# Attention in groups of 256 queries instead of 512: the order of first pass, turns and transfers in a transformer layer

## The chip, the cores and the metric

One core of one Trainium2 chip runs the kernel. The metric is the device time of one execution in microseconds; the kernel before takes 524.16 us, the median of three runs (523.96 to 524.35). The engines are TensorE (PE; its weight loads stand as PEld), VectorE (DVE), ScalarE (ACT), GpSimd (POOL) and SyncE (SP), which here only issues transfers.

## What is computed

The reference, cut to what matters. The input has 2 batches of 1024 positions of 512 features.

```python
def layer(x):                       # (2, 1024, 512)
    qk = (x @ Wqk.T + bqk).reshape(b, n, 8, 8, 2)   # 8 heads of 8 features
    q, k = qk[..., 0], qk[..., 1]
    v = x @ Wv.T + bv
    attn = softmax(q @ k.T) / sqrt(64)              # 1024 x 1024 per head
    x = layernorm(x + (attn @ v) @ Wo.T + bo)
    g, u = x @ Wg.T, x @ Wu.T                       # int4 weights, scales per 128 inputs, 1792 wide
    return layernorm(x + (silu(g) * u) @ Wd.T)
```

## The kernel before

**Blocks and groups.** The 2048 queries are four blocks of 512. Eight heads fall into two groups of four, so there are 8 attention groups of 512 queries and four heads; each goes over 1024 keys in 8 steps of 128 keys, 64 steps in all (`ALL`).

**First pass.** Softmax needs the largest score of each query first. A unit (L911) multiplies 128 queries of one head by 512 keys into one of three PSUM banks, the ring, and VectorE reduces it to a maximum per query (L1198). There are 256 units, 32 for a group (`FG`). When a group's units are done VectorE combines the two halves of the keys (L1206), GpSimd splits the maxima into three half-precision parts (L537), TensorE turns them into rows (a turn "M", L927), ScalarE copies these out of PSUM (L736), and SP moves them into the query operand (`max_rows`, L421), where they are subtracted within the scores product itself. The scores of a group wait for that transfer (L988).

**Second pass.** A step n has two pairs. A pair is two scores products (L981), of two heads at once on two halves of TensorE's rows, and one exponential of 1024 columns (L721). The AV product of the step before (L1017) follows in two halves of 256 columns. Scores alternate between two pairs of PSUM banks, and all "turns" take one of these places too: the maxima's turn M, the turn of a finished group's AV product (avT, behind a copy, L724), which VectorE then normalises (L1216), that of the attention (attT) and the output projection (wo). `turns_at` (L262) says at which step each stands.

**How the two passes run together.** Before the first step TensorE does `AHEAD` = 46 units; then each pair brings two more (L1060 to L1067). So units run out at step `DRAIN` = 53 of 64, and the rest of the loop takes the work of blocks 1 and 2 that was set aside (`ASIDE`, L282): their attention turns and output projections, added by VectorE (L1288). Ahead of the first step TensorE also has, by the hand-written list `later` (L1051), the projections of batch 1 in 12 chunks (L847, L857) and the placement of batch 0's query and key rows: 12 products (L895) that sort features by head, each followed by a ScalarE copy into the stack (L705). The second 512 queries of batch 0 and all rows of batch 1 are placed by transfers instead (`place_second_half`, L412; `place_rows`, L345).

**Queues.** Each engine does its instructions in order. SP: the inputs, the second half's queries, row transfers of groups 0 and 1, batch 1's placements, x's first half, and so on (L436 to L480). GpSimd: fills and constants, splits of the maxima, the scaling of batch 1's queries and keys into high and low parts (L552), half of batch 1's placements, bias additions to x, and the loads of the feed-forward weights, each of which waits for a group's rows to land (L563).

**Behind attention.** VectorE normalises block 0's rows, GpSimd splits them in two half-precision parts, SP transposes them by transfer (L459), and the feed-forward starts (L1126); its first gate product waits for these transposes, for the additions set aside and for the normalisation. SP's transposes stand behind the store of the down-projection's scale ratios, which VectorE computes (L1269). The feed-forward of the other blocks follows period by period without a break.

## Time and profile before

| | |
|---|---|
| median of 3 runs | 524.16 us |
| the profiled execution, its span | 523.78 us, 521.7 us |
| mean granted TensorE clock | 0.992 of full speed |
| TensorE, VectorE, ScalarE, GpSimd busy | 498.3, 413.5, 405.8, 247.9 us |
| 256 first-pass reduces (L1203) | 157.1 us busy |
| 128 exponentials (L721) | 140.6 us busy |
| feed-forward gate, up and down products (L1084, L1096, L1111) | 115.5, 115.3, 131.5 us busy |

Busy time is the union of an engine's instructions. Times in rows count from the span's start. A bracket behind a row is the time that the engine sat idle before it, and who ended that. A row with xN merges N instructions that follow one another. Beside SP stands the time in which it issues transfers; their landing is later.

### The profile page before, as it was taken

To read this page: it belongs to the slowest core of one execution; us is meant where nothing else is said; L and a number is where in the kernel's file an instruction comes from. 1 tells how busy PE (TensorE), PEld (TensorE's weight loads), DVE (VectorE), ACT (ScalarE), POOL (GpSimd) and SP (SyncE) were. 2 spreads that over 40 slices of the span, in tenths; PEclk is the share of its full clock that TensorE was granted. 3 is DMA by queue.
4 is the path that set the end of the run, shared out by engine and by line. 5 is a ranking of instruction groups with operands and counts; after the bars stand their busy time and mean duration, and the time that the engine had idled before them with its cause. 6 is when DMAs were issued, how large, how long until landed. Compare 5 with 4: busy or idle time off the path is not lost.

```text
span 521.7 us, 8074 instructions
## 1 busy us (share of the span) xinstructions
PE 498.3 (96%) x2976; PEld 192.6 (37%) x2976; DVE 413.5 (79%) x706; ACT 405.8 (78%) x558; POOL 247.9 (48%) x288
## 2 busy tenths in 40 slices
PE   8899999999999999999999999999999999999991
PEld 3222232322222222334444444444444444444440
DVE  3699999989999996368778778777668666677677
ACT  1523789998899889877888888888888888888860
POOL 9100091833100625072564686656874834637744
PEclk9999999999999999999999999999999999999996
DMA  6510018675620007400031121130020020000202
GB/s 191 158 45 9 18 42 210 193 142 108 105 44 1 3 5 180 183 0 1 1 62 21 21 41 21 29 54 1 1 80 1 0 82 0 2 1 1 80 0 80
DMA packets 30006, 28.93 MB, mean 55 GB/s; under 512 B 19472, under 2 KB 21904, under 8 KB 29712
## 3 DMA queue, kind: packets, MB, share of 16 engines
q1 hardware_dynamic: 26544, 22.40, 15.2%
q0 software_dynamic: 3424, 6.03, 6.4%
q8 instruction: 23, 0.38, 0.3%
q14 instruction: 15, 0.12, 0.1%
HBM read 24.10 MB, written 4.22 MB: 54 GB/s over the span
## 4 chain that ended last, share of the span: by engine, by line
PE 85%; DVE 7%; ACT 5%; issue 2%; DMA 1%; POOLq 0%; DVEq 0%; POOL 0%; SPq 0%; ACTq 0%
PE ps L1084 18%; PE ps L1096 18%; PE ps L1111 18%; PE ps L1029 9%; PE ps L1000 6%; PE ps L924 6%; DVE mxh L1203 4%; ACT pbuf L721 3%; PE ps L853 3%; PE ps L1012 1%; PE ps L863 1%; PE ps L977 1%; PE ps L907 1%; DMA arena<-xT 1%; ACT avt L728 1%
## 5 line engine op out<-in xcount | busy, mean ns | idle before, releaser
L1203 DVE TENSOR_REDUCE mxh<-ps 128x1 f32<-128x512 f32 x256 | 157.1, 681 | 6.5 <-PE ps L924 5.1
L721 ACT ACTIVATE pbuf<-ps,gamma 128x1024 f32<-128x1024 f32 x128 | 140.6, 1115 | 16.1 <-PE ps L1000 11.2
L802 ACT ACTIVATE ps<-ps,ratio 128x512 f32<-128x512 f32 x168 | 106.5, 659 | 40.3 <-PE ps L1084 37.3
L1111 PE MATMUL ps<-wd,stack 128*128 128x512 f16 x448 | 131.5, 379 | 0.7 <-POOL stack L643 0.7
L1368 DVE TENSOR_TENSOR ps<-ps,stack 128x512 f32<-128x512 f32 x128 | 88.2, 695 | 36.1 <-PE ps L1111 34.3
L1084 PE MATMUL ps<-arena,wg 128*128 128x512 f16 x448 | 115.5, 379 | 0.1
L1096 PE MATMUL ps<-arena,wu 128*128 128x512 f16 x448 | 115.3, 379 | 0.1
L808 ACT ACTIVATE ps<-ps,ratio 128x512 f32<-128x512 f32 x156 | 98.9, 659 | 5.5 <-PE ps L1096 1.1
L641 POOL CAST stack<-pbuf 128x512 f16<-128x512 f32 x56 | 34.2, 611 | 91.6 <-DVE pbuf L1352 91.6
L1368 DVE TENSOR_TENSOR ps<-ps,pbuf 128x512 f32<-128x512 f32 x80 | 55.0, 696 | 23.2 <-PE ps L1111 22.4
L1029 PE MATMUL ps<-pbuf,arena 128*32 128x256 f32 x832 | 66.5, 391 | 1.7 <-ACT avt L728 1.7
L643 POOL TENSOR_TENSOR stack<-pbuf,stack 128x512 f16<-128x512 f32 x56 | 64.8, 1158 | 4.5
L1111 PEld LDWEIGHTS ps<-wd,stack 128*128 128x128 f16 x448 | 43.7, 98 | 54.0 <-POOL stack L643 1.3
L1084 PEld LDWEIGHTS ps<-arena,wg 128*128 128x128 f16 x448 | 43.2, 98 | 54.9 <-ACT pbuf L816 1.7
L1096 PEld LDWEIGHTS ps<-arena,wu 128*128 128x128 f16 x448 | 43.7, 98 | 53.3 <-DVE pbuf L1352 2.0
L924 PE MATMUL ps<-stack 64*128 64x512 f16 x256 | 60.8, 381 | 1.4 <-DVE mxh L1203 0.7
L543 POOL CAST mp<-mx 128x16 f16<-128x16 f32 x8 | 1.6, 197 | 107.5 <-DVE mx L1213 107.5
L1000 PE MATMUL ps<-stack 64*128 64x512 f16 x256 | 49.6, 386 | 1.9 <-ACT pbuf L721 1.6
L1352 DVE SCALAR_TENSOR_TENSOR pbuf<-ps,scales,pbuf 128x512 f32<-128x512 f32 x56 | 41.9, 748 | 6.6 <-PE ps L1096 6.5
L816 ACT ACTIVATE pbuf<-ps,scales 128x512 f32<-128x512 f32 x56 | 38.1, 680 | 0.2 <-PE ps L1084 0.2
L1000 PEld LDWEIGHTS ps<-stack 64*128 64x128 f16 x256 | 12.3, 92 | 58.2 <-issue 37.5
L924 PEld LDWEIGHTS ps<-stack 64*128 64x128 f16 x256 | 20.9, 94 | 34.2 <-DVE mxh L1203 31.2
(112 smaller groups left out, 368.5 us busy)
## 6 DMA issues: line engine op xcount, KB each, us to landing
arena<-xT SPq DMA_DIRECT2D x16, 256.0 KB, 5.4
x<-x SPq DMA_DIRECT2D x2, 2048.0 KB, 9.4
out<-x SPq DMA_DIRECT2D x3, 1024.0 KB, 4.2
stack<-down_ratios SPq DMA_DIRECT2D x1, 2048.0 KB, 7.4
wg<-gq POOLq DMA_DIRECT2D x4, 448.0 KB, 7.4
wu<-uq POOLq DMA_DIRECT2D x4, 448.0 KB, 7.3
wd<-dq POOLq DMA_DIRECT2D x2, 896.0 KB, 10.5
pbuf<-down_ratios SPq DMA_DIRECT2D x1, 1536.0 KB, 6.1
```

The source lines that it names most:

```text
L643: nc.gpsimd.tensor_tensor(mparts[:, 1, t % NM, :], sg[t % 2], mparts[:, 0, t % NM, :], ALU.subtract)\
L721: nc.scalar.activation(pbuf[:, pi % 4, :].rearrange("p (a n) -> p a n", a=2), ps[:, at:at + 2, :], ACT.Exp, scale=gamma[:, n // (ALL // B) ...
L802: nc.scalar.activation(gbank[t % 2], gbank[t % 2], ACT.Copy, scale=gr[:, t % G, c:c + 1])\
L808: nc.scalar.activation(ubank[t % 2], ubank[t % 2], ACT.Copy, scale=ur[:, t % G, c:c + 1])\
L924: nc.tensor.matmul(ring_bank("first", n), qs[b][rows, k, t, qt * P:(qt + 1) * P], ks[b][rows, t, half * TB:(half + 1) * TB], start=True, s ...
L1000: mm = nc.tensor.matmul(bank[at + j], ks[b][rows, t, kt * P:(kt + 1) * P], qs[b][rows, k, t, :], start=True, stop=True)
L1029: mm = nc.tensor.matmul(bank[AVB][j * VC:(j + 1) * VC, lo:hi], vst[b][:, kt, g * HG + j, :], pbuf[:, (2 * n + j // 2) % 4, (j % 2) * TB + ...
L1084: mm = nc.tensor.matmul(gbank[t % 2], wg[:, c, i * P:(i + 1) * P], x1v[blk][:, a, c, :, :], start=(c == 0 and a == 0), stop=(a == 1), skip ...
L1096: mm = nc.tensor.matmul(ubank[t % 2], wu[:, c, i * P:(i + 1) * P], x1v[blk][:, a, c, :, :], start=(c == 0 and a == 0), stop=(a == 1), skip ...
L1111: mm = nc.tensor.matmul(bank[k], mparts[:, a, t % NM, k * P:(k + 1) * P], wd[:, i, :], start=(i == 0 and a == 0), stop=(a == 1), skip_grou ...
L1203: nc.vector.tensor_reduce(mxh[:, f % 2, qh, half:half + 1], ring_bank("first", n), AX.X, ALU.max)\
L1368: nc.vector.tensor_tensor(dst, bank[k], down_row(i), ALU.mult).then_inc(s_dr[k], 1)
```

## The change

Groups become 256 queries: 16 groups of 16 units, each over 1024 keys in 4 steps of 256 keys, 64 steps as before. The scores of a pair become four products of 256 columns, an AV call sums 128 keys for all 256 queries. Attention starts behind 30 units, the first pass ends at step 57 of 64. There are 16 turns of the maxima, each of four row transfers of half the size; the AV turns stay 8, each of two groups, normalised together. The query and key rows of heads in the last two positions of batch 0's first 512 queries are placed by 32 transfers (keys on SP, queries on GpSimd) instead of 6 products and copies, into memory that GpSimd clears first. x is loaded by GpSimd's queue, its bias added in eighths, the feed-forward weights in six parts. On SP batch 1's placements stand behind group 2's rows, and on VectorE the order behind the first pass is new. The diff, cut to its core:

```diff
-NG = H // HG
-STEPS = NG * KT
+QB = 2
+QT = BT // QB
+QN = TB // QB
+GROUPS = H // HG * QB
+NF = NB * GROUPS
+TURNS = NF // QB
+KS = KT // 2
+STEPS = GROUPS * KS
...
-FG = HG * BT * 2
-FIRST = NB * NG * FG
+MQ = HG * QT
+FG = 2 * MQ
+FIRST = NF * FG
...
-            f, r = divmod(n + 3, KT)
-            if r == 0 and f < NB * NG:
+            f, r = divmod(n + 3, KS)
+            if r == 0 and f < NF:
...
-            f, r = divmod(n - 9, KT)
-            if r == 0 and 0 <= f < LASTF:
-                return [("avT", f, 0)]
+            a, r = divmod(n - 10, QB * KS)
+            if r == 0 and 0 <= a < TURNS - 1:
+                return [("avT", a, 0)]
...
-            if r == 2:
+            if r == 3:
...
-        WO_AT = (3, 4)
-        LASTF = NB * NG - 2
-        DRAIN = ALL - 11
-        ASIDE = {DRAIN: ("attT", 1, 0), DRAIN + 1: ("wo", 1, 0), DRAIN + 3: ("wo", 1, 1), DRAIN + 4: ("avT", LASTF, 0),
-                 DRAIN + 6: ("attT", 2, 0), DRAIN + 7: ("wo", 2, 0), DRAIN + 9: ("wo", 2, 1)}
+        WO_AT = (4, 7)
+        DRAIN = ALL - 7
+        ASIDE = {DRAIN: ("attT", 1, 0), DRAIN + 1: ("wo", 1, 0), DRAIN + 2: ("wo", 1, 1), DRAIN + 3: ("attT", 2, 0),
+                 DRAIN + 4: ("wo", 2, 0), DRAIN + 5: ("wo", 2, 1)}
...
-        copied = [use for use in aside for _ in range({"avT": 0, "attT": 1, "wo": 2}[use[0]])]
+        copied = [use for use in aside for _ in range({"attT": 1, "wo": 2}[use[0]])]
...
-        placed = [use for t in range(TH) for use in ((1, 0, t), (0, 0, t), (1, 1, t))]
+        placed = [use for t in range(2) for use in ((1, 0, t), (0, 0, t), (1, 1, t))]
...
+        def place_last_heads(engine, kind):
+            for jj in range(2):
+                for part in range(2):
+                    at = kind * HD + jj * HD // 2
+                    for slot in range(4)[half_slots(kind, part)]:
+                        r = ROWS * jj + E * slot
+                        for t in range(2, TH):
+                            src = (high, low)[part][at + t:at + HD // 2:TH, :]
+                            if kind:
+                                engine.dma_start(ks[0][r:r + E, t, :], src).then_inc(s_late[kind], 16)
+                            else:
+                                engine.dma_start(qs[0][r:r + E, 0, t, :], src[:, 0:TB]).then_inc(s_late[kind], 16)
...
             def max_rows(f):
-                u, g = divmod(f, NG)
+                u, q4 = divmod(f, GROUPS)
+                g, h = divmod(q4, QB)
...
-                for jj in range(2):
-                    r = ROWS * jj + MROW
-                    sp.dma_start(qs[b][r:r + 3, k, 2 * g:2 * g + 2, :],
-                                 mrows[6 * BT * jj:6 * BT * (jj + 1), f % 2, :]).then_inc(s_mld[g], 16)
-            sp.wait_ge(s_fill, 7)
+                for c in range(HG):
+                    r, t = ROWS * (c // 2) + MROW, 2 * g + c % 2
+                    sp.dma_start(qs[b][r:r + 3, k, t, h * QN:(h + 1) * QN],
+                                 mrows[3 * QT * c:3 * QT * (c + 1), f % 2, :]).then_inc(s_mld[q4], 16)
+            sp.wait_ge(s_fill, 11)
...
+            place_last_heads(sp, 1)
+            max_rows(0)
...
-            max_rows(0)
...
+            max_rows(2)
...
-            sp.dma_start(x1[:, 0:8, :], x[0:8].rearrange("t p n -> p t n")).then_inc(s_x[0], 16)
-            max_rows(2)
-            for jj in range(2):
-                sp.wait_ge(s_stk1[jj], 16 * PARTS)
-            sp.wait_ge(s_vt, B)
-            sp.dma_start(x1[:, 8:16, :], x[8:16].rearrange("t p n -> p t n")).then_inc(s_x[1], 16)
-            max_rows(3)
             def turn_x1(u):
...
-            for f in range(4, NB * NG):
+            for f in range(3, NF):
...
-                if f == 5:
+                if f == 10:
...
+            nc.gpsimd.memset(qs[0][:, 0, 2:TH, :].bitcast(F32), 0.0).then_inc(s_fill, 1)
+            nc.gpsimd.memset(ks[0][:, 2:TH, :].bitcast(F32), 0.0).then_inc(s_fill, 1)
+            pool.wait_ge(s_fill, 9)
+            for jj in range(2):
+                r = ROWS * jj + MROW
+                nc.gpsimd.memset(ks[0][r:r + 3, 2:TH, :].bitcast(F32), MINUS_ONES).then_inc(s_fill, 1)
...
-            pool.wait_ge(s_fill, 6)
+            pool.wait_ge(s_fill, 11)
+            pool.wait_ge(s_high, 1)
+            pool.wait_ge(s_low, 1)
+            place_last_heads(pool, 0)
             def second_batch_parts():
...
+                for late in s_late:
+                    pool.wait_ge(late, 16 * 16)
...
             def load_weights(f):
-                pool.wait_ge(s_mld[f % NG], 16 * 2 * (f // NG + 1))
-                if f == 2:
-                    for c in range(C):
-                        pool.dma_start(wg[:, c, :], gq[c]).then_inc(s_gu, 16)
-                if f == 3:
-                    for c in range(C):
-                        pool.dma_start(wu[:, c, :], uq[c]).then_inc(s_gu, 16)
-                if f == 4:
-                    for g in range(0, G, G // 2):
-                        pool.dma_start(wd[:, g:g + G // 2, :], dq[g:g + G // 2].rearrange("g p n -> p g n"))\
-                            .then_inc(s_dq, 16)
+                pool.wait_ge(s_mld[f % GROUPS], 16 * HG * (f // GROUPS + 1))
+                half, kind = (f - 4) % 2, (f - 4) // 2
+                if kind < 2:
+                    for c in range(2 * half, 2 * half + 2):
+                        pool.dma_start((wg, wu)[kind][:, c, :], (gq, uq)[kind][c]).then_inc(s_gu, 16)
+                else:
+                    own = slice(half * G // 2, (half + 1) * G // 2)
+                    pool.dma_start(wd[:, own, :], dq[own].rearrange("g p n -> p g n")).then_inc(s_dq, 16)
...
+            def load_x(b):
+                if b:
+                    for half in s_stk1:
+                        pool.wait_ge(half, 16 * PARTS)
+                    pool.wait_ge(s_vt, B)
+                own = slice(b * N // P, (b + 1) * N // P)
+                pool.dma_start(x1[:, own, :], x[own].rearrange("t p n -> p t n")).then_inc(s_x[b], 16)
...
+            load_x(0)
+            split_max(2)
...
+            split_max(3)
...
             def add_attention(u, t):
...
-                pool.wait_ge(s_xb, u * TB // N + 1)
+                pool.wait_ge(s_xb, 2 * (u + 1))
...
-            def add_bias(b):
+            def add_bias(i):
...
-                pool.wait_ge(s_x[b], 16)
-                half = x1[:, b * N // P:(b + 1) * N // P, :]
-                nc.gpsimd.tensor_tensor(half, half, bo_s.unsqueeze(1).to_broadcast([P, N // P, D]), ALU.add)\
-                  .then_inc(s_xb, 1)
-            for f in range(2, NB * NG):
+                pool.wait_ge(s_x[i // BT], 16)
+                two = x1[:, 2 * i:2 * i + 2, :]
+                nc.gpsimd.tensor_tensor(two, two, bo_s.unsqueeze(1).to_broadcast([P, 2, D]), ALU.add).then_inc(s_xb, 1)
+            for f in range(4, NF):
...
-                if f == 2:
-                    add_bias(0)
-                if f in (2, 3, 4):
+                for i in {4: (0,), 5: (1,), 6: (2,), 10: (3,), 12: (4, 5), 13: (6,), 14: (7,)}.get(f, ()):
+                    add_bias(i)
+                for t in {7: (0, 1), 8: (2, 3)}.get(f, ()):
+                    add_attention(0, t)
+                if 4 <= f < 10:
...
-                if f == 6:
-                    add_bias(1)
-                if f == 3:
-                    for t in range(BT):
-                        add_attention(0, t)
+                if f == 9:
+                    load_x(1)
...
             def av_out(f):
-                act.wait_ge(s_av, 2 * (f + 1) * KT)
+                act.wait_ge(s_av, 2 * (f + 1) * KS)
...
-                    act.wait_ge(s_of, turn_count["avT", f - 2, 0])
-                nc.scalar.activation(avt[:, f % 2, :], bank[AVB], ACT.Copy).then_inc(s_ave, 1)
+                    act.wait_ge(s_of, turn_count["avT", f // QB - 1, 0])
+                h = f % QB
+                nc.scalar.activation(avt[:, f % 2, :], bank[AVB][:, h * QN:(h + 1) * QN], ACT.Copy).then_inc(s_ave, 1)
             def first_max_out():
...
-                nc.scalar.activation(mrows[:, 0, :], ring_bank("M", 0)[0:3 * HG * BT, :].bitcast(F16)[:, 0:P],
...
-            for n in range(4, 9):
+            for n in range(4, 6):
...
-            for n in range(9, 11):
-                keep(n)
...
-            keep(11)
...
-                    if pair and n and n % KT == 0:
-                        av_out(n // KT - 1)
+                    if pair and n and n % KS == 0:
+                        av_out(n // KS - 1)
...
-            av_out(NB * NG - 1)
+            av_out(NF - 1)
...
-                    pe.wait_ge(s_kept, 3 * t + 2 + half)
+                    if t < 2:
+                        pe.wait_ge(s_kept, 3 * t + 2 + half)
+                    else:
+                        for late in s_late:
+                            pe.wait_ge(late, 16 * 16)
...
             def scores(n, pair):
...
-                g, kt = divmod(s, KT)
+                q4, kp = divmod(s, KS)
+                g, h = divmod(q4, QB)
...
-                if kt == 0 and pair == 0:
-                    pe.wait_ge(s_mld[g], 16 * 2 * (u + 1))
+                if kp == 0 and pair == 0:
+                    pe.wait_ge(s_mld[q4], 16 * HG * (u + 1))
...
-                for j in range(2):
-                    rows, t = slice(ROWS * j, ROWS * (j + 1)), 2 * g + pair
-                    mm = nc.tensor.matmul(bank[at + j], ks[b][rows, t, kt * P:(kt + 1) * P],
-                                          qs[b][rows, k, t, :], start=True, stop=True)
+                for kk in range(2):
+                    kt = 2 * kp + kk
+                    for j in range(2):
+                        rows, t = slice(ROWS * j, ROWS * (j + 1)), 2 * g + pair
+                        mm = nc.tensor.matmul(bank[at + j][:, kk * QN:(kk + 1) * QN], ks[b][rows, t, kt * P:(kt + 1) * P],
+                                              qs[b][rows, k, t, h * QN:(h + 1) * QN], start=True, stop=True)
...
-            def av_whole(n):
+            def av(n, kk):
...
-                mm.then_inc(s_av, 2)
-            def av(n, half):
-                u, s = divmod(n, STEPS)
-                g, kt = divmod(s, KT)
-                b = u * TB // N
+                q4, kp = divmod(s, KS)
+                g, h = divmod(q4, QB)
+                b, kt = u * TB // N, 2 * kp + kk
...
-                if kt == 0 and n:
-                    pe.wait_ge(s_ave, n // KT)
-                lo, hi = half * TB // 2, (half + 1) * TB // 2
+                if kp == 0 and n:
+                    pe.wait_ge(s_ave, n // KS)
...
-                    mm = nc.tensor.matmul(bank[AVB][j * VC:(j + 1) * VC, lo:hi], vst[b][:, kt, g * HG + j, :],
-                                          pbuf[:, (2 * n + j // 2) % 4, (j % 2) * TB + lo:(j % 2) * TB + hi],
-                                          start=(kt == 0 and half == 0), stop=(kt == KT - 1), skip_group_check=True)
+                    lo = (j % 2) * TB + kk * QN
+                    mm = nc.tensor.matmul(bank[AVB][j * VC:(j + 1) * VC, h * QN:(h + 1) * QN], vst[b][:, kt, g * HG + j, :],
+                                          pbuf[:, (2 * n + j // 2) % 4, lo:lo + QN],
+                                          start=(kt == 0), stop=(kt == KT - 1), skip_group_check=True)
...
-            later = {1: [(put, 3)], 3: [turn_v], 5: [(put, 4)], 7: [(put, 5)], 9: [(put, 6)], 11: [second[0]],
-                     13: [(put, 7)], 15: [second[1]], 17: [second[2]], 19: [(put, 8)], 21: [second[3]], 23: [second[4]],
-                     25: [(put, 9)], 27: [second[5]], 29: [second[6]], 31: [(put, 10)], 33: [second[7]], 35: [second[9]],
-                     37: [(put, 11)], 40: [second[10]], 42: [second[8]], 44: [second[11]], 46: [second[12]]}
+            later = {0: [(put, 3)], 2: [turn_v], 4: [(put, 4)], 6: [(put, 5)], 8: [second[0]], 10: [second[1]],
+                     12: [second[2]], 13: [second[3]], 15: [second[4]], 17: [second[5]], 18: [second[6]], 20: [second[7]],
+                     23: [second[9]], 25: [second[10]], 26: [second[8]], 28: [second[11]], 30: [second[12]]}
...
-                av_whole(n - 1)
-            av_whole(ALL - 1)
+                for kk in range(2):
+                    av(n - 1, kk)
+            for kk in range(2):
+                av(ALL - 1, kk)
...
-                nc.vector.tensor_tensor(mx[:, f % 2, :], mxh[:, f % 2, :, 0], mxh[:, f % 2, :, 1], ALU.max)\
+                nc.vector.tensor_reduce(mx[:, f % 2, :], mxh[:, f % 2, :, :], AX.X, ALU.max)\
...
-                if n == 38:
+                if n == 24:
...
-            for n in range(ALL):
+            for n in range(DRAIN):
...
-            for k in range(BT):
+            for k in range(2):
+                attention_stats(0, k)
+            att_out(1)
+            for k in range(2, BT):
...
-            att_out(1)
-            down_ratios()
+            normalise(TURNS - 2)
...
+            for t in range(2, BT):
+                add_output(1, t)
+            att_out(2)
+            down_ratios()
+            for t in range(2):
+                add_output(2, t)
...
-                add_output(1, t)
-            normalise(LASTF)
-            att_out(2)
-            for t in range(BT):
```

## Rows read from the trace of the kernel before

**Rows 1.** Page, part 2: TensorE's busy tenths in 40 equal slices of the span

```profile
PE   8899999999999999999999999999999999999991
```

**Rows 2.** Stretches: us; busy us of PE, PEld, DVE, ACT, POOL (instructions); clock; DMA; GB/s

```profile
130.00:140.00 10.00, 9.54 (x98) 2.79 (x91) 9.65 (x17) 9.23 (x11) 1.93 (x2) 1.00 0.48 71
...
200.00:210.00 10.00, 9.75 (x70) 2.48 (x68) 4.34 (x9) 9.49 (x11) 2.64 (x3) 1.00 0.93 266
```

**Rows 3.** Timeline, VectorE's reduces: at the start of attention, and one unbroken run

```profile
51.27 2.48 DVE L1203 TENSOR_REDUCE mxh<-ps 128x1 f32<-128x512 f32 x4 [0.31 <-PE ps L924]
...
68.32 8.46 DVE L1203 TENSOR_REDUCE mxh<-ps 128x1 f32<-128x512 f32 x14 [0.31 <-PE ps L924]
```

**Rows 4.** Timeline behind the last reduce, and the transposes' issues (lowest/median/highest)

```profile
188.44 0.17 DVE L1213 TENSOR_TENSOR mx<-mxh 128x16 f32<-128x16 f32 x1
...
191.63 0.27 DVE L1272 TENSOR_TENSOR stack<-stack 128x112 f32<-128x112 f32 x1
...
193.17 1.28 DVE L1293 TENSOR_TENSOR x<-ps,x 128x512 f32<-128x512 f32 x2
...
194.36 3.04 DVE L1251 TENSOR_SCALAR x<-x,mv,rstd 128x512 f32<-128x512 f32 x4
...
215.15 0.60 PE L1084 MATMUL ps<-arena,wg 128*128 128x512 f16 x2
...
L465 SPq DMA_TRANSPOSE arena<-split x16: 1232/1233/1756, 197.6 to 347.7; - x16
```

**Rows 5.** Timeline ahead of attention, TensorE (start, duration, instruction, waits before it)

```profile
20.64 0.39 PE L924 MATMUL ps<-stack 64*128 64x512 f16 x2 [0.46 <-ACT stack L713]
...
33.38 1.13 PE L853 MATMUL ps<-arena,wqk_s 128*128 128x512 f32 x2
34.44 0.39 PE L924 MATMUL ps<-stack 64*128 64x512 f16 x2
...
34.76 1.08 PE L863 MATMUL ps<-arena,wv_s 128*64 128x512 f32 x4
...
50.63 0.39 PE L1000 MATMUL ps<-stack 64*128 64x512 f16 x2
```

**Rows 6.** SP's issues (first, and lowest/median/highest of L356), and two pairs of scores

```profile
22.01 5.87 SPq L419 DMA_DIRECT2D stack<-x  x8
...
L356 SPq DMA_DIRECT2D stack<-x x8: 671/672/1434, 71.9 to 77.7; - x8
...
62.88 0.39 PE L1000 MATMUL ps<-stack 64*128 64x512 f16 x2
...
82.65 0.39 PE L1000 MATMUL ps<-stack 64*128 64x512 f16 x2
```

**Rows 7.** Timeline: SP issues a group's rows; GpSimd's next issue waits for their landing

```profile
110.39 1.47 SPq L433 DMA_DIRECT2D stack<-mrows  x2
...
113.38 2.17 POOL L571 DMA_DIRECT2D wu<-uq  x4 [5.82 <-DMA stack<-mrows]
```

**Rows 8.** Timeline of one turn of the maxima, 84.7 to 92.7 us, TensorE and VectorE

```profile
84.73 0.17 DVE L1213 TENSOR_TENSOR mx<-mxh 128x16 f32<-128x16 f32 x1
...
87.08 0.24 PE L930 MATMUL ps<-ident,mp 128*48 128x128 f16 x1
...
88.69 9.90 DVE L1203 TENSOR_REDUCE mxh<-ps 128x1 f32<-128x512 f32 x16 [0.20 <-PE ps L924]
...
92.72 0.39 PE L1000 MATMUL ps<-stack 64*128 64x512 f16 x2
```

**Rows 9.** Timeline: VectorE behind an AV copy, and one AV call of 256 columns

```profile
76.93 1.29 DVE L1203 TENSOR_REDUCE mxh<-ps 128x1 f32<-128x512 f32 x2 [0.15 <-PE ps L924]
...
88.59 0.64 PE L1029 MATMUL ps<-pbuf,arena 128*32 128x256 f32 x8
```

**Rows 10.** Table of DMA issues: KB each and median us from issue to landing

```profile
arena<-split SPq DMA_TRANSPOSE x16, 3.0
...
down_ratios<-stack SPq DMA_DIRECT2D x1, 28.0 KB, 2.0
```

72 lines of the change are left out of this document (32 added, 40 removed).

## The prediction

> **What bounds the kernel now.** I read the page's slices first [rows 1]: TensorE is called busy in nearly all of them, but the ends of its matmuls are modelled, so this alone says little. The table of stretches [rows 2] separates two regimes. In the attention loop (130 to 140 us) VectorE works 9.65 of 10 us beside TensorE's 9.54 and ScalarE's 9.23, at a granted clock of 1.00. The timeline shows who sets the pace there: 14 row-maximum reduces take 8.46 us [rows 3], 0.60 each; a step of the loop carries four, 2.39 us. From 200 us, with the reduces done (the last ends at 188.44), VectorE is at 4.34 of 10, and scores, exponentials, AV products and the output projections set aside for this stretch run on to 215.15 [rows 4], the first gate product. From there to the end the feed-forward keeps TensorE at 9 tenths in every slice; the change alters nothing in it. So the change is worth what it moves the 215.15.
>
> The sum has two parts: when VectorE ends its 256 reduces, and how long attention goes on after that. It is made against the profiled execution's 523.78 us, 0.38 below the median of the three runs, 524.16.
>
> **The change, part by part.**
>
> *Start.* Attention begins at unit 30 in place of 46. Now the first unit stands at 20.64 us and the first scores at 50.63 [rows 5]. Between them TensorE must still do all of batch 1's projections; of nine later placements three stay. Its work: 30 units in pairs, 15 by 0.32 us (34.44 to 34.76), 4.8; twelve chunks of projection by 1.06 (33.38 to 34.44), 12.7; three placements and three turns at half a chunk each, an estimate, 3.2; and 1.7 of waits for ScalarE's copies at its head, estimated from the 0.46 that the first unit waits. 20.6 + 22.4 = 43.0 us, 7.6 earlier. VectorE needs for 30 units and one row maximum 18.7 us and, begun 0.4 behind the first unit, would be done at 39.8; the denser chunks starve it, so it loses about 3.4 us there. Now it has 46 units, the maximum and a combine behind it at 51.27 [rows 3], 28.5 us of work in 30.2, 1.7 lost. **The reduce stream ends about 2.0 later** (between 0, were the chunks hidden, and 3.5).
>
> The last heads' sixteen key transfers go through SP, their sixteen query transfers through GpSimd. SP pays 5.87 us for eight such issues, 0.73 each, at worst 1.43 [rows 6]; GpSimd 0.54 [rows 7]. SP is free at 22.0, so again at 33.7; the first maxima are ready near 37.5, and four issues (3.0) and a landing (1.5) bring them at 42, behind the chunks. GpSimd's sixteen, 9 us, begin behind its longer fills, near 18.5, and end before the first maxima, near 32. Batch 0's other placements and their copies go from engines that the loop does not wait for there. All this I cost at nothing; its cover is those chunks.
>
> *Turns of the maxima.* Sixteen groups need eight more turns while reduces run. What one costs stands in [rows 8]: a combine of 0.17 and the break it makes in the stream, 0.20 in all; then the turn (87.08) takes a scores bank, the next scores wait for the exponential just before, and VectorE waits 0.20 behind a reduce of 0.68 whose pitch is 0.60 otherwise, 0.28 lost. **8 by 0.48 is +3.8.** The combine becomes a reduction over pairs of 16 numbers, which no row shows; it lies between nothing and a whole reduce, 0.68, and is nearest to the old combine by elements. Bounds: 1.6 (bubble hidden) to 6.
>
> *AV copies.* Sixteen halves for eight wholes. Beside a copy and its turn VectorE now waits 0.15 [rows 9], by pitch 0.23 lost, six times, 1.4. A half holds TensorE up for less, so I leave 0.05 for each of 14 and 0.28, as for a maxima's turn, for each of the six AV turns, which stand by themselves now: 2.4, **+1.0** (0 to 3). The normalisations stay eight of the same shape.
>
> *Scores in halves.* Four matmuls of 256 columns per pair for two of 512: the columns are the same, two weight loads are added. No row shows it; between nothing and 0.1 per pair. TensorE has that to spare beside VectorE's 1.20 per pair except behind some 20 bubbles: **+0.5** (0 to 2.5).
>
> *SP's queue.* Four row transfers per group, 3.0 us of issues where two take 1.47. From a turn (87.08) to the next group's scores (92.72) are 5.64 us [rows 8]. Rows land 1.5 us behind the last issue (113.38 against 111.86, [rows 7]), 4.1 behind the turn; then 5.6. The slack shrinks from 1.5 to nearly nothing; behind a late row stands TensorE, and behind it VectorE, which has 0.6 to 1 us of units in hand. I cost it at nothing for that cover. But SP also issues batch 1's twelve placements, 12 by 0.73 and one dear issue, 9.4 us, and these now stand right ahead of group 3's rows. They begin, as now, 9.0 us behind the pair in which the scales are cast (62.88 to 71.9, [rows 6]), so group 3's rows land 9.0 + 9.4 + 3.0 + 1.5 = 22.9 behind it. Its scores come seven and a half steps behind that pair, 19.8 us now (62.88 to 82.65) and some 0.7 more with one turn more. TensorE stands 2.4 us, VectorE about **+1.7** (0 to 3.5). The Trainium skill ("DMA: Bandwidth & Descriptors", Issuing engines are not separate DMA queues) calls the sequencer's time to initiate a transfer usually small beside the transfer; by that SP would be through in time and the sum 1.7 less. The 0.73 per issue speaks against it here.
>
> *GpSimd.* Bias additions in eighths, x's two issues and the weight loads lie between the splits of the maxima; the weight loads wait for a group's rows and then have about 1 us to the next split. Nothing, while rows land in time; a late row would delay the next split too.
>
> Reduces end at 188.4 + 2.0 + 3.8 + 1.0 + 0.5 + 1.7 = **197.4**.
>
> *Drain.* Seven steps instead of eleven, but all four output halves, two attention turns, an AV turn and a maxima's turn stay in it. TensorE: 28 AV and scores calls, 14 by 0.64 [rows 9] and 14 by about 0.25, 12.5; four output halves by about 1.06 like a chunk, 4.2; turns 1.9; 18.6, then the last exponential and waits for the first maxima and for VectorE's first addition, some 2.5: 21.1. Beside it runs the feed-forward's own input. VectorE's new order puts the statistics, one copy, the normalisation (behind the AV turn at 5.3) and two additions ahead of the norm's application, which begins at 7.2 and takes 3.0 [rows 4]; two additions (1.3), a copy (0.5) and the down ratios (191.63 to 193.17, 1.6) end at 13.6. SP stores these (2.0, [rows 10]) before it may transpose block 0: the fourth transpose goes out three issues of 1.23 later and lands 3.0 after that: 22.3. Today's application begins at 194.36, so its transposes land well ahead of the 215.15; that cover is gone. I take **22.0** (20 to 24) against 26.7.
>
> Feed-forward at 197.4 + 22.0 = 219.4, 4.2 later than 215.15: **523.8 + 4.2 = 528.0 us**.
>
> **Rivals.** 0.2%, about 1 us, is what a measurement of this kernel can tell from no change.
> - *Faster*: VectorE never idles at a turn, as TensorE and ScalarE, busy 9.54 and 9.23 of 10 us [rows 2], have slack to make up a bubble. Then the loop costs the start's 2.0 and the combines' 1.6 alone: 192.0 + 22.0 = 214.0, 1.15 earlier: 522.6. It decides where VectorE's gap at the new turns and at group 3 stays under 0.05. Against it: the gap at today's turns. 0.20.
> - *About even*: the placements leave SP in time and the drain is 20.0: 528.0 - 1.7 - 2.0 = 524.3. Its first half is what the Trainium skill's page on DMA, named above, would give. 0.12.
> - *Much slower*: a group's rows land after its scores want them, 1.2 late with 0.6 covered, at 12 groups: 7.2 more, 535.2. For it the slack of nearly nothing, against it today's 1.5. 0.10.
> - *The start is not early*: at 1.43 an issue SP is free at 45, the first rows land at 49 and 6.3 is lost, 534.3. The change would not do what it says. 0.05.
> - The forecast, 525.4 to 532.5: 0.53.
>
> **Numbers.** Half of the fast and of the slowest cases left out, the range is 521.6 to 532.5. Slower 0.53 + 0.10 + 0.05 = 0.68, same 0.12, faster 0.20.
>
> **What would show it.** Right: first scores near 43 us; a VectorE gap of about 0.2 at each of some 14 maxima's turns; SP still issuing placements when group 3's maxima are read, and TensorE standing there; the last reduce near 197; block 0's last transpose landing within 1 us of the first gate product, near 219. Wrong: a last reduce before 193, or less than 19 us from it to the first gate product.

## The result, and the profile after

The changed kernel takes **540.24 us** (538.67 to 540.52, four runs) where the kernel before took 524.25 in the same comparison (523.96 to 524.61, four runs): ratio 1.0297, 95% interval 1.0281 to 1.0313. The forecast was 528.0, with a range of 521.6 to 532.5. The direction was right, the size was not: 16 us in place of 4. The time of a kernel here and below is the median of its executions; one execution of the kernel called e16 below took 976.33 us, and nothing on record shows why. The profiled execution took 540.52 us, its span is 538.5, and all lines of "after" below are from it.

The page shows little of it. TensorE's slices [rows 1] have some eights and sevens in the first half where there were nines, and a stretch in which nothing is late (130 to 140 us) is as in [rows 2]. The last reduce now lies at 207. Page, TensorE's tenths:

```profile
PE   8798897999988998899999999999999999999991
```

A stretch of after, in the columns of [rows 2]:

```profile
130.00:140.00 10.00, 9.68 (x117) 3.59 (x113) 9.76 (x18) 9.15 (x11) 4.23 (x7) 1.00 0.46 90
```

The ends that the forecast works with are read from the timeline of after: the first unit, the first scores, the combine right behind the last reduce, and the first gate product, which answer to [rows 5] and [rows 4]:

```profile
22.61 0.51 PE L958 MATMUL ps<-stack 64*128 64x512 f16 x1
...
45.42 0.39 PE L1038 MATMUL ps<-stack 64*128 64x256 f16 x4
...
207.12 0.17 DVE L1240 TENSOR_REDUCE mx<-mxh 128x8 f32<-128x16 f32 x1
...
231.97 0.59 PE L1111 MATMUL ps<-arena,wg 128*128 128x512 f16 x2 [0.30 <-DMA arena<-split]
```

The gate product is 16.8 later than the 215.15 of before, and from it to the end both spans have 306.5 us: the whole loss lies ahead of the feed-forward. The last reduce is 18.7 later than before, the drain 1.9 shorter (24.9 for 26.7). First scores are 5.2 earlier, though the first unit stands 2.0 later.

Who waited for whom, TensorE, first lines (total, times, longest):

```profile
PE ps L1038 <- DMA stack<-mrows: 9.1, 3, 4.2
PE ps L1038 <- ACT pbuf L753: 4.4, 13, 0.4
PE ps L1012 <- DVE x L1319: 3.1, 2, 2.5
```

The top line does not exist before: three times TensorE stands at a group's first scores for the maxima's rows. The timeline of after has these three places, with what was issued ahead of them:

```profile
48.57 0.98 POOL L607 DMA_DIRECT2D x<-x  x1
...
51.07 2.99 SPq L453 DMA_DIRECT2D stack<-mrows  x4
...
58.66 0.39 PE L1038 MATMUL ps<-stack 64*128 64x256 f16 x4 [1.91 <-DMA stack<-mrows]
...
68.74 5.72 SPq L360 DMA_DIRECT2D stack<-x  x8
74.51 2.79 SPq L357 DMA_DIRECT2D stack<-x  x4
...
77.47 0.39 PE L1038 MATMUL ps<-stack 64*128 64x256 f16 x4
...
77.82 3.01 SPq L453 DMA_DIRECT2D stack<-mrows  x4
...
83.98 0.39 PE L1038 MATMUL ps<-stack 64*128 64x256 f16 x4 [4.16 <-DMA stack<-mrows]
...
149.63 0.92 POOL L607 DMA_DIRECT2D x<-x  x1
...
155.02 2.91 SPq L453 DMA_DIRECT2D stack<-mrows  x4
...
162.63 0.44 PE L1038 MATMUL ps<-stack 64*128 64x256 f16 x4 [2.99 <-DMA stack<-mrows]
```

Groups 1, 3 and 10. From the end of the last issue to the scores are 4.6, 3.2 and 4.7 us (58.66 less 54.06, 83.98 less 80.83, 162.63 less 157.93), where [rows 7] had 1.5. A step of the loop runs from one scores call to the next of its kind: step 11 takes 83.98 - 77.47 = 6.51, steps 3 and 39 take 4.71 and 5.45, where most steps take 2.3 to 3.0.

The stretches around the waits of groups 1 and 3 (columns as above; the last but one is the busy share of the DMA engines) show a second cost:

```profile
56.30:58.60 2.30, 0.45 (x8) 0.00 (x0) 1.23 (x3) 0.52 (x1) 0.00 (x0) 1.00 0.64 240
58.60:60.60 2.00, 1.78 (x20) 0.67 (x20) 1.29 (x2) 1.50 (x2) 0.00 (x0) 1.00 0.00 0
...
80.00:83.90 3.90, 0.00 (x0) 0.00 (x0) 0.61 (x2) 0.13 (x1) 0.00 (x0) 1.00 0.27 39
83.90:85.60 1.70, 1.62 (x14) 0.41 (x14) 0.85 (x2) 1.11 (x1) 0.00 (x0) 0.63 0.00 0
85.60:87.60 2.00, 2.00 (x18) 0.49 (x14) 1.48 (x4) 1.11 (x1) 1.06 (x5) 0.50 0.00 0
```

At group 3 TensorE did nothing for 3.9 us, and afterwards its granted clock is 0.50 (1.2 GHz of 2.4): step 12 takes 3.66 us. Behind group 10 it is the same (step 40: 3.74). In the first experiment below, where no scores wait for rows, both take 2.39. Behind group 1's wait the clock stayed at 1.00.

### The profile page after: what moved, and what is told of

It reads as the page before. It is cut to its first block, busy times and chain, and to the rows that moved or that the text cites. A ratio compares the mean times of both kernels' runs of the same rounds, so it can differ in the third digit from the quotient of the medians.

```text
span 538.5 us, 8976 instructions
## 1 busy us (share of the span) xinstructions
PE 500.9 (93%) x3324; PEld 205.9 (38%) x3324; DVE 417.0 (77%) x714; ACT 404.3 (75%) x568; POOL 267.8 (50%) x348
## 4 chain that ended last, share of the span: by engine, by line
PE 79%; DVE 6%; DMA 5%; SPq 4%; ACT 3%; issue 2%; POOL 1%; POOLq 0%; DVEq 0%; ACTq 0%
PE ps L1111 18%; PE ps L1123 18%; PE ps L1138 17%; PE ps L1055 8%; PE ps L1038 6%; PE ps L958 5%; DMA stack<-mrows 3%; ACT pbuf L753 3%; PE ps L883 3%; SPq L453 1%; PE ps L893 1%; DMA arena<-xT 1%; SPq L360 1%; DVE mxh L1230 1%; PE ps L937 1%
## 5 line engine op out<-in xcount | busy, mean ns | idle before, releaser
L1055 PE MATMUL ps<-pbuf,arena 128*32 128x256 f32 x1024 | 82.6, 400 | 1.1 <-ACT pbuf L753 1.0
L1038 PE MATMUL ps<-stack 64*128 64x256 f16 x512 | 50.8, 277 | 14.0 <-DMA stack<-mrows 9.1
L958 PE MATMUL ps<-stack 64*128 64x512 f16 x256 | 61.1, 388 | 0.8 <-DVE mxh L1230 0.8
L562 POOL CAST mp<-mx 128x8 f16<-128x8 f32 x16 | 3.0, 190 | 89.1 <-DVE mx L1240 89.1
L1038 PEld LDWEIGHTS ps<-stack 64*128 64x128 f16 x512 | 15.4, 95 | 70.0 <-issue 36.0
L1055 PEld LDWEIGHTS ps<-pbuf,arena 128*32 128x32 f32 x1024 | 21.6, 109 | 30.9 <-issue 17.7
```

Source lines behind the costliest of these rows:

```text
L958: nc.tensor.matmul(ring_bank("first", n), qs[b][rows, k, t, qt * P:(qt + 1) * P], ks[b][rows, t, half * TB:(half + 1) * TB], start=True, s ...
L1038: mm = nc.tensor.matmul(bank[at + j][:, kk * QN:(kk + 1) * QN], ks[b][rows, t, kt * P:(kt + 1) * P], qs[b][rows, k, t, h * QN:(h + 1) * QN ...
L1055: mm = nc.tensor.matmul(bank[AVB][j * VC:(j + 1) * VC, h * QN:(h + 1) * QN], vst[b][:, kt, g * HG + j, :], pbuf[:, (2 * n + j // 2) % 4, l ...
```

## The experiments

Nine questions, each told with the time of its kernel beside the 540.24 of after; the kernel before was run beside all of them, at 523.9 to 524.2.

**How much do the rows cost?** The rows go to a spare tile and no scores wait for them.

```diff
-  sp.dma_start(qs[b][r:r + 3, k, t, h * QN:(h + 1) * QN], mrows[...])
+  sp.dma_start(aside_rows[r:r + 3, q4, c % 2, :], mrows[...])
-  if kp == 0 and pair == 0: pe.wait_ge(s_mld[q4], 16 * HG * (u + 1))
-  ... ACT.Exp, scale=gamma[...]
+  ... ACT.Exp, scale=flat[:]
```

> The changed kernel, with the maxima's rows sent (same transfers, same order, same sizes) to a spare buffer, so that no scores wait for them; the maxima are thus left out of the scores, and the exponentials get a scale of 0 to stay finite. Theory (rows that land after their scores want them cost the most of what the forecast missed): the three long steps of the changed kernel (3, 11 and 39: 4.71, 6.51 and 5.45 us against 2.39 to 2.87) and the slow step behind each are gone, worth 1.8 + 4.9 + 3.9 = 10.6; the last reduce ends near 197 instead of 207.12, the time is 529 to 532. Rival (the reduces are what counts, TensorE's stalls are only where their lateness shows): VectorE stays busy elsewhere, the last reduce ends after 203 and the time is above 535.

528.93 us, 11.3 less. Timeline, behind the last reduce and at the first gate product:

```profile
194.60 0.17 DVE L1243 TENSOR_REDUCE mx<-mxh 128x8 f32<-128x16 f32 x1
...
219.29 0.59 PE L1113 MATMUL ps<-arena,wg 128*128 128x512 f16 x2 [1.78 <-DMA arena<-split]
```

The theory holds; the gain is a little above what it gave (194.6 where it had 197, 528.9 where it had 529 to 532). The profiled execution took 527.95, 1.0 below the median. From the first reduce to the last combine are 172.28 us (22.32 to 194.60), before 167.37 (21.07 to 188.44): eight more turns, the halves and the shorter start cost 4.9 together, where the forecast had 7.3. The gate product now waits 1.78 for block 0's transposes.

**What delays them: the bytes beside them, or GpSimd's queue?** First, x by SyncE at the same moments.

```diff
   place_second_half()
+  load_x(sp, 0)
...
   max_rows(f)
+  if f == 9: load_x(sp, 1)
```

> The changed kernel with x's two 2 MB loads issued by SyncE again, at the same points of the loop (the first behind the second half's placements, the second behind the rows of group 9). Theory A (any 2 MB load that is under way delays rows that are sent beside it): groups 1 and 10 stay late, by as much or more since their rows now stand behind x in the same queue; 540 to 545. Theory B (it is GpSimd's queue that delays them): rows of groups 1 and 10 land 1.5 to 3 us behind their last issue, steps 3 and 39 take 2.4 to 2.9, and the time is 534.5 to 536.5. Group 3's stall stays in either.

536.66, at the edge of what theory B gave and below theory A, though neither holds as it stands: group 1 is as late as before its move (step 3: 4.66; 1.86 of wait), and at group 10 the wait shrinks (step 39: 3.68). Timeline of this run:

```profile
52.06 2.99 SPq L462 DMA_DIRECT2D stack<-mrows  x4
...
59.61 0.39 PE L1038 MATMUL ps<-stack 64*128 64x256 f16 x4 [1.86 <-DMA stack<-mrows]
```

So rows are late without GpSimd's queue too: at group 1 it makes no difference which of the two engines issued the 2 MB (4.6 us from the last issue to the scores in both), though in this run the rows also stand behind x in SyncE's own queue. The Trainium skill's page "DMA: Bandwidth & Descriptors", section "Issuing engines are not separate DMA queues", says that transfers of all engines run on the same 16 DMA engines and interleave; group 1 agrees. At group 10 SyncE issued x 1.4 us earlier than GpSimd had (148.19 for 149.63) and the rows 0.7 later (155.72 for 155.02), so less of the load was left, and TensorE waits 1.22 in place of 2.99; that this is the whole of it is not shown.

Then x in eighths, behind rows that have landed.

```diff
   split_max(1)
-  load_x(0)
+  pool.wait_ge(s_mld[1], 16 * HG)
+  for i in range(2): load_x(i)
...
   place_rows(pool, 0)
+  for i in range(2, 4): load_x(i)
...
-  if f == 9: load_x(1)
+  if 10 <= f < 14: pool.wait_ge(s_mld[f % GROUPS], ...); load_x(f - 6)
```

> The changed kernel with x loaded in eighths of 0.5 MB, still by GpSimd: two behind the landing of group 1's rows, two behind GpSimd's placements of batch 1, and one behind the landing of the rows of each of the groups 10 to 13; the additions of the bias follow their eighths. Theory (it is the bytes under way beside them that keep rows from landing): steps 3 and 39 fall from 4.71 and 5.45 us to 2.3 to 2.9, group 3's stall stays, and the time is 534 to 536.5. Rival (rows of these groups are late by their issues alone): both steps stay above 4 us and the time above 538.5.

537.65, 1 us above the expectation. Steps 3 and 39 are plain again, but group 3's grew from 6.51 to 8.87. Timeline of this run:

```profile
76.97 3.01 SPq L453 DMA_DIRECT2D stack<-mrows  x4
...
78.25 1.49 POOL L607 DMA_DIRECT2D x<-x  x2
...
85.48 0.61 PE L1043 MATMUL ps<-stack 64*128 64x256 f16 x4 [6.50 <-DMA stack<-mrows]
```

Two eighths of x, 1 MB, were now issued beside group 3's rows, and these came 5.5 us behind their last issue. The load took its delay along to where it was put, so it is the load beside them that makes the rows late.

**Does the kernel before stand it?** There, x by GpSimd at the places of the change.

```diff
   split_max(1)
+  pool.dma_start(x1[:, 0:8, :], ...).then_inc(s_x[0], 16)
...
   load_weights(4)
+  pool.dma_start(x1[:, 8:16, :], ...).then_inc(s_x[1], 16)
```

> The kernel before, with x's two loads issued by GpSimd at the places that the change gives them: behind the split of group 1's maxima, and behind the second half of the down weights. Theory (a 2 MB load delays rows sent beside it, and the kernel before has 1.5 us of slack per group): group 1's rows land about 3 us later, TensorE stands 1 to 2 us at its first scores, and the time is 524.5 to 526.5. Rival (the slack and the units in hand cover it): within 0.3 us of the kernel before.

527.51; ratio 1.0062 (1.0047 to 1.0078), 1 us above the expectation.

```profile
65.40 1.15 POOL L574 DMA_DIRECT2D x<-x  x1
...
68.21 1.48 SPq L433 DMA_DIRECT2D stack<-mrows  x2
...
75.08 0.61 PE L1001 MATMUL ps<-stack 64*128 64x512 f16 x2 [2.26 <-DMA stack<-mrows]
```

5.4 us from the last issue to the scores, in a kernel that lacks every other part of the change. This one part of the change costs 3.3 us by itself; its second load meets no late row.

In all four places (groups 1 and 10 of after, group 3 with the eighths, and here) the rows come about when the load stops. In after the busy share of the DMA engines falls to 0.00 at 58.6 us and from 0.84 to 0.03 at 162.6, as the scores of groups 1 and 10 begin; in the run with eighths it is 0.55 from 83 to 85 and 0.00 from there, here 0.92 from 72 to 74 and 0.39 from 74 to 76, with placements under way. The kernel before has the same 2 MB beside rows without harm: x's first half goes out at 81.33, group 2's rows 6.9 us later, at 88.18, and their scores at 92.72 wait for nothing. At groups 1 and 10 of after and here the rows went out 2.5, 5.4 (with 0.9 MB of weights ahead of x) and 2.8 us behind x. As far as these rows show, 4.6 to 5.5 us is what was left of a load, and not a price of the transfer.

**Group 3: the order of SyncE's queue?** Its rows between the query and the key placements of batch 1.

```diff
-  place_rows(sp, 1)
+  place_rows(sp, 1, (0,))
+  max_rows(3)
+  place_rows(sp, 1, (1,))
```

> The changed kernel with group 3's four row transfers put between SyncE's eight query and four key placements of batch 1, instead of behind all twelve. Theory (they are late for standing in that queue): their first issue moves from 77.82 to the turn's copy, about 74.7, step 11 falls from 6.51 us to under 3.5 and the time to 535 to 537. Rival (they land late because GpSimd's twelve placements, issued from 72.54 to 79.1 and landing until 83.4, fill the queues): step 11 stays above 5.5 and the time within 1 us of the changed kernel's.

535.11, 5.1 less. Step 11 is 3.21 us:

```profile
74.47 3.40 SPq L453 DMA_DIRECT2D stack<-mrows  x4
...
80.36 0.39 PE L1040 MATMUL ps<-stack 64*128 64x256 f16 x4 [0.85 <-DMA stack<-mrows]
```

**Would more time do instead?** Four units more ahead, and the maxima's turn a step earlier.

```diff
-AHEAD = FG + 14
+AHEAD = FG + 18
...
-  f, r = divmod(n + 3, KS)
+  f, r = divmod(n + 4, KS)
...
-  DRAIN = ALL - 7
+  DRAIN = ALL - 8
...
```

> The changed kernel with attention beginning at unit 34 in place of 30 and the maxima's turn a step earlier, four steps ahead of their group; eight steps instead of seven behind the last reduce. Theory (the rows have too little time between the turn and the scores): every group has a step, some 2.4 us, more; group 1's stall goes, those of groups 3 and 10 shrink to under 2.5 and 1.5 us, the last reduce ends at 199 to 201 and the drain is 1.5 to 2 us longer: 533.5 to 536.5. Rival (the stalls do not depend on when the maxima are turned, since the queues are full): three stalls of the same size and 541 to 543.

533.57, 6.7 less. TensorE's wait for rows falls from 9.1 to 3.7 (twice, the longest 3.1, where the theory had under 2.5), the last reduce ends at 198.9, and the drain is 1.6 longer (26.4). Both signs are as the theory had them: time ahead is bought with drain.

**The drain: the down ratios.** Five small operations of VectorE go back ahead of GpSimd's splits.

```diff
   mean_variance(0)
+  down_ratios()
   normalise(TURNS - 2)
...
   att_out(2)
-  down_ratios()
```

> The changed kernel with VectorE's five operations for the down ratios put right behind the first block's mean and variance, ahead of the last normalisations but one, instead of between block 2's copy and its first additions. Theory (beside GpSimd's splitting of block 0 they take 3.9 us instead of 1.6, and both the last output half on TensorE and block 0's transposes wait for them): they take 1.6 to 2 again, step 62 falls from 6.77 us to under 4.5 and the time to 536.5 to 538.5. Rival (the drain is bound by TensorE's own work or by GpSimd's splits): under 1 us is gained.

535.69, 4.6 less, 0.8 us more than the most that was expected; the drain takes 20.4. In the timeline of after, VectorE and GpSimd, and what waited:

```profile
219.69 1.27 DVE L1303 TENSOR_TENSOR stack<-stack 128x112 f32<-128x112 f32 x1
...
221.53 1.20 DVE L1307 TENSOR_TENSOR stack<-stack 128x56 f32<-128x56 f32 x1
222.65 1.28 DVE L1319 TENSOR_TENSOR x<-ps,x 128x512 f32<-128x512 f32 x2
...
219.66 1.16 POOL L625 TENSOR_TENSOR split<-x,split 128x512 f16<-128x512 f32 x1
...
221.50 1.15 POOL L625 TENSOR_TENSOR split<-x,split 128x512 f16<-128x512 f32 x1
...
222.76 0.34 SPq L488 DMA_DIRECT2D down_ratios<-stack  x1
224.28 5.52 SPq L478 DMA_TRANSPOSE arena<-split  x4
...
224.07 1.92 PE L1012 MATMUL ps<-wo_s,attT 64*128 64x512 f32 x4 [2.46 <-DVE x L1319]
```

And in this experiment:

```profile
211.33 0.28 DVE L1303 TENSOR_TENSOR stack<-stack 128x112 f32<-128x112 f32 x1
...
212.18 0.22 DVE L1307 TENSOR_TENSOR stack<-stack 128x56 f32<-128x56 f32 x1
...
227.97 0.60 PE L1111 MATMUL ps<-arena,wg 128*128 128x512 f16 x2
```

L1303 takes 1.27 or 0.28, L1307 1.20 or 0.22: begun beside a GpSimd operation of the same moment, each lasts until that one ends (220.96 and 220.82; 222.73 and 222.65). The Trainium skill, "SBUF — State Buffer", section "Who interferes with whom", has it that VectorE and GpSimd contend only for one shared pair of ports, which is an exclusive lock, and that a VectorE operation with two operands in SBUF contends with a GpSimd one that reads SBUF; the rows beside the splits agree. Not every GpSimd operation does this: in this experiment a GpSimd operation on 4 columns (L553) runs from 211.29 to 212.33, and L1303 beside it takes its 0.28.

**The start.** Two of the four new fills by VectorE at its very start, then all four.

```diff
+  nc.vector.memset(qs[0][:, 0, 2:TH, :]...); nc.vector.memset(ks[0][:, 2:TH, :]...)
...
-  nc.gpsimd.memset(qs[0][:, 0, 2:TH, :]...); nc.gpsimd.memset(ks[0][:, 2:TH, :]...)
```

> The changed kernel with the two new fills of the last heads' columns done by VectorE at its very start, where it waits for the first transfers, instead of by GpSimd beside the first scales. Theory (VectorE's small operations take 0.97 us instead of 0.16 beside a GpSimd fill, and TensorE's clock falls to one half behind the longer pause): the integer operation on the scale row takes 0.16 again, the first reduce starts at 21 to 21.5 us instead of 23.16, and the time falls by 1 to 2 us, 538 to 539.5. Rival (the loop absorbs it): the first reduce is earlier and the time within 0.5 us of the changed kernel's.

> The changed kernel with all four new fills of the last heads' columns on VectorE at its start, the two of minus ones too, so that GpSimd is idle from 14.6 us as in the kernel before. Theory (a small operation of VectorE waits until the GpSimd fill beside it ends): the two operations on the scale row take 0.16 each, the first reduce starts near 21.3 us, 1 to 1.9 earlier than in the changed kernel, and the time is 538 to 539.5. Rival (the start is late for its transfers): first reduce above 22.5 us.

With two, 540.42, no gain: GpSimd's two remaining fills moved up and ended at 16.61, still beside the scale row, and the first reduce began at 23.14. With all four, 539.65: the first reduce at 21.32, 1.8 earlier, the time 0.6 less. Timeline of after, then of the kernel with four:

```profile
15.70 0.22 DVE L1195 TENSOR_SCALAR row<-row 1x2 f32<-1x2 f32 x1
15.96 0.97 DVE L1199 TENSOR_SCALAR row<-row 1x2 int32<-1x2 int32 x1
...
15.97 1.94 POOL L546 MEMSET stack<- 3x1024 f32 x2
```

```profile
15.62 0.16 DVE L1198 TENSOR_SCALAR row<-row 1x2 f32<-1x2 f32 x1
15.81 0.16 DVE L1202 TENSOR_SCALAR row<-row 1x2 int32<-1x2 int32 x1
```

The mechanism holds, its worth does not follow. Group 1's scores come 2.1 earlier (56.56 for 58.66), but the two steps behind them take 4.19 and 3.80 where after has 2.87 and 3.01, at a granted clock of 0.50 from 58.5 to 62.5 us, and step 6 begins at 64.54 in both kernels. TensorE still waits 8.1 us for rows, and 1.0 of the 1.8 is left at the last reduce. In after the fills do not slow everything beside them: VectorE's next two operations, L1201 and L1202, take 0.15 and 0.13 beside the second.

**The price of the scores in halves**, alone, in the kernel before.

```diff
-  nc.tensor.matmul(bank[at + j], ks[...], qs[b][rows, k, t, :])
+  for lo in range(0, TB, TB // 2):
+      nc.tensor.matmul(bank[at + j][:, lo:lo + TB // 2], ks[...], qs[b][rows, k, t, lo:lo + TB // 2])
```

> The kernel before, with each scores product of 512 columns issued as two of 256, and nothing else changed: the price of the scores in halves by itself. Forecast's term: +0.5 us, 524.5. Rival 1: nothing (TensorE has the time beside VectorE's reduces), within 0.2 of the kernel before. Rival 2: two more weight loads per pair, behind every bubble and in the eleven steps of the drain: +2 to +4.

524.61; ratio 1.0007 (0.9998 to 1.0016), that is, -0.1 to +0.8 us. The forecast's 0.5 and nothing both fit; the second rival falls.

**Do the places add up?** The edits of groups 1 and 10, of group 3, of the drain and two fills together; then with all four fills.

> The changed kernel with four edits together: group 3's rows between SyncE's placements, the down ratios early, x in eighths behind landed rows, and the two fills by VectorE. Theory (these four places are all that the forecast missed, and they add up): 5.1, 4.5, 4 to 5 and 1 to 2 off 540.2, thus 523.5 to 526.5, first gate product at 215 to 218, no step of the loop above 4 us. Rival (one stall hides another, so the gains overlap): above 528.

> The four edits together, with all four fills on VectorE. Theory: as with four, 525.25, less the 0.8 to 1.3 us of the start: 523.8 to 524.6, even with the kernel before. Rival: the start is lost again at the first scores, 525.2.

525.25 (ratio 1.0021, 1.0010 to 1.0033) and 525.42. They add up, and gain 15.0 where the four by themselves gained 12.1 (5.1 + 4.6 + 2.6 - 0.2), mostly because the eighths of x no longer meet late rows at group 3 (step 11: 3.26, and 8.87 with the eighths alone). With all four fills, the rival of the second text came true: the last 0.8 of the start came back as a wait of 2.14 at group 3 (step 11: 4.50). Three kernels asked what held these rows now, SyncE's eight placements ahead of them or x beside them:

```diff
 e13                          e14                                  e15
-  place_rows(sp, 1, (0,))      place_rows(pool, 0)                  both
   max_rows(3)                + pool.wait_ge(s_mld[3], 16 * HG)
-  place_rows(sp, 1, (1,))      for i in range(2, 4): load_x(i)
+  place_rows(sp, 1)
```

> The five edits, with all twelve of SyncE's placements behind group 3's rows instead of eight ahead and four behind. If the placements ahead in the same queue keep these rows: step 11 falls from 4.50 us to under 3.0 and the time from 525.4 to 522.5 to 524. If it is x's eighths beside them: step 11 stays above 4 us and the time at 525 or more.

> The five edits, with x's third and fourth eighth issued when group 3's rows have landed instead of right behind GpSimd's placements; SyncE's order stays (eight placements, the rows, four placements). If x's bytes keep the rows: step 11 under 3.0 us, 522.5 to 524. If the placements ahead in the queue do: step 11 above 4 us, 525 or more.

> Both of these: group 3's rows ahead of all SyncE's placements and of x's third and fourth eighth. Theory: no step of the loop above 3.5 us, last reduce at 194 to 195, first gate product near 214.7, 522.5 to 523.8, below the kernel before by 0.1 to 0.3%. Rival: rows land late for GpSimd's own twelve placements beside them, step 11 above 4 us, 525.

524.67, 525.44 and 524.36. Without x beside them step 11 stays at 4.23; without the placements ahead it is plain, but group 4 stands instead (step 15: 4.06 in e13, 4.21 in e15, where no step was to be above 3.5), whose rows SyncE could not issue before 82.71. The profiled executions of the kernel with all five edits, of e14 and of e15 lie 0.8, 0.7 and 1.5 us above their medians, so these steps may be dearer than usual; by the medians x beside the rows is worth nothing, and the placements ahead 0.8. Timeline of e13:

```profile
70.59 2.91 SPq L453 DMA_DIRECT2D stack<-mrows  x4
73.60 6.16 SPq L360 DMA_DIRECT2D stack<-x  x8
79.81 2.79 SPq L357 DMA_DIRECT2D stack<-x  x4
82.71 2.98 SPq L453 DMA_DIRECT2D stack<-mrows  x4
...
87.78 0.39 PE L1040 MATMUL ps<-stack 64*128 64x256 f16 x4 [1.60 <-DMA stack<-mrows]
```

So the twelve were divided, four and eight, or six and six.

```diff
-  place_rows(sp, 1, (0,)); max_rows(3); place_rows(sp, 1, (1,))
+  place_rows(sp, 1, slice(0, 6)); max_rows(3); place_rows(sp, 1, slice(6, 12))
```

> The five edits, with four of SyncE's twelve placements ahead of group 3's rows and eight behind. If the order of the queue is all: both step 11 and step 15 under 3.3 us (the eight are issued by 79.3, ahead of group 4's turn near 82), last reduce near 194, 522.8 to 523.8. If the placements' bytes delay whichever rows come next: one of the two steps stays at 4 us, 524.5 to 525.5.

> The same with six ahead and six behind. If the order of the queue is all: as e16, within 0.5 us of it. If bytes delay the rows: step 11 between 3.3 and 4.5 us, 524 to 525.5.

523.43 (e16) and 523.49 (e17); ratios 0.9988 (0.9979 to 0.9996) and 0.9987 (0.9978 to 0.9995). Waits for rows are down to 0.5 us and less, the ends of e17 are

```profile
194.71 0.17 DVE L1252 TENSOR_REDUCE mx<-mxh 128x8 f32<-128x16 f32 x1
...
215.08 0.60 PE L1116 MATMUL ps<-arena,wg 128*128 128x512 f16 x2
```

and both versions are below the kernel before by 0.6 us, hardly more than the interval. That is what the order of the queue alone would give: step 11 takes 2.70 and 2.86, step 15 2.39 in both.

## Why the prediction was wrong

Its sum put the last reduce at 197.4; it ends at 207.1. The 9.7 are: +10.0 rows, +2.1 start, -2.4 loop.

- **Rows (failed).** The step "I cost it at nothing for that cover", for four transfers per group that land 1.5 behind their last issue. The 1.5 was read at one group [rows 7] whose rows went out just as a load ended: the busy share of the DMA engines there is 1.05 from 108 to 110 us and 0.04 from 112 to 114. Beside 1 to 3 MB that were still to move it was 4.6 to 5.5. The paragraph on GpSimd costed x in its queue at "Nothing, while rows land in time", and so never asked what the loads do to the rows. Without any wait for rows the stream ends 11.7 earlier at the same start (207.1 less 194.6, less 0.8 of start); 1.7 of it was foreseen. TensorE's waits are 9.1 of the 11.7, and half clock behind groups 3 and 10 is 2.4: steps 11 to 13 and 39 to 41 take 13.01 and 12.04, without waits 7.68 and 7.78, and the waits in them are 4.16 and 2.99.
- **Group 3 (mechanism right, size off).** The queue was named, TensorE's stand there too; TensorE was to stand 2.4 us and stood 4.16, plus about 1.2 at half clock in the steps behind. Landing was put at 1.5 and took 3.2, and the 0.7 that VectorE's units in hand were to cover were not there: it idled 4.14 beside the 4.16.
- **The start (half right).** From first unit to first scores 22.8, forecast 22.4. But the first unit was kept at 20.64: of the new fills the text says only that GpSimd's placements begin behind them. They stood beside VectorE's scale row, 0.9 us there; the first placements then ran at a granted clock of 0.50 to 0.53, 0.7 more (in the run of the drain's experiment, behind the same pause, at 1.00); the rest is x's columns, which landed 0.3 later.
- **Turns, copies, halves (a little too dear).** 7.3 with the start's 2.0, measured 4.9 in the kernel that waits for no rows. VectorE's gap at a turn is 0.20 to 0.21, as said.
- **The drain (failed at one term).** 22.0 forecast, 24.9 measured, 20.4 with the ratios early. The failed term is the down ratios at 1.6, read ahead of GpSimd's splits [rows 4], which began there at 194.97: beside them they take 3.9 (218.72 to 222.65). That moved the transposes and the last output half on TensorE, which then ran at a granted clock of 0.57 (stretch of 224 to 228 us). That block 0's transposes set the end, with no cover left, was right for after: the gate product waits 0.30 for them, and 1.78 in the first experiment. With the ratios early it waits for nothing that its row shows.

Of the rivals, "much slower" had the cause, late rows, but as a little at each of 12 groups; it was much at three, each beside a load or behind a queue. "Faster" was approached only by the repaired kernel (523.4 where it had 522.6), with a drain of 20.4 in place of 22.0; the loop costs more than it allowed even there (from the first reduce to the last combine 5.5 more than before in e17, where it had 3.6). The rule on the time to initiate a transfer, from the Trainium skill's page on DMA named above, was weighed against the 0.73 per issue in the forecast and set aside; the runs bear that out, since the placements hold up whichever rows come behind them in SyncE's queue.

## What to carry to other kernels

A landing time belongs to the traffic beside it: before a transfer with little slack is costed at nothing, list the loads that will be under way while it lands, the ones that the same change moves above all, and ask when each will be through. Where an order within one queue decides, look for the next customer too, since a delay taken from one group came up at the next until the placements were divided. A small operation of VectorE can cost the rest of the GpSimd operation beside it, and a gain ahead of a wait for DMA is worth little until that wait is gone (0.6 of 1.8 us here).

## What was not expected of the hardware

- Transfers of a few rows between two places of SBUF took 1.3 to 1.5 us from their last issue where no load was left to move (86.15 to 87.43 with four edits; [rows 7]), 2.1 to 3.8 behind or beside a dozen small placements, and 4.6 to 5.5 beside loads of 1 to 3 MB. At group 1 it was 4.6 whichever engine issued the load.
- A VectorE operation on 2 numbers took 0.97 us for 0.16, one on 112 columns 1.27 for 0.28, by ending with the GpSimd operation beside it; other operations beside GpSimd kept their time.
- A wait of 4.16 us on TensorE was followed by some 3.6 us at half clock, which cost 1.2 us beyond the wait. Behind waits of 1.91 (group 1 of after) and of 3.05 (group 10 with group 3's rows moved) the granted clock stayed at 1.00, behind one of 1.78 (group 1 with all fills on VectorE) it fell to 0.50: the length of the wait alone does not tell which.
